# A four-stage graph and expert network on one core: the search for entries above one moves from the first stage to the last, and the general path moves behind it

## What is computed

```python
x = x + L0_gnn(layernorm(x), adj)   # e = leaky_relu(f1_i + f2_j); where(adj > 0, e, -9e15); softmax; @ h; elu
x = x + L0_ffn(layernorm(x))        # 8 experts, the best 2 for each row, gelu, hidden 256
x = x + L1_gnn(layernorm(x), adj)   # alpha = where(adj == k, leaky_relu((h * a_{k-1}) @ h.T), -9e15) for k = 1..4; softmax; @ h
x = x + L1_ffn(layernorm(x))        # 8 experts for every row, three products, weights from the mean over the batches
```

## Time and profile before

| what | us |
|---|---|
| three runs | 1109.86, 1111.55, 1112.64 (median 1111.55) |
| the profiled execution | 1111.38 |
| its span, first to last instruction | 1109.6 |
| stage A (0 to about 290), B (to 456.1), C (460.65 to 757.1), D (757.2 to the end) | 290, 166, 296, 352 |
| busy PE, PEld, DVE, ACT, POOL | 1028.1, 745.1, 685.0, 766.2, 383.6 |

### The profile page before, as it was taken

How to read it: one execution, slowest core, us unless ns; L and a number is a source line. 1 busy time by engine, 2 the same in 40 slices (tenths; PEclk the granted TensorE clock), 3 DMA queues, 4 the chain that set the end, 5 groups by cost and what they waited for, 6 DMA issues and landing times. The chain is left out here.

```text
span 1109.6 us, 20053 instructions
## 1 busy us (share of the span) xinstructions
PE 1028.1 (93%) x6445; PEld 745.1 (67%) x6445; DVE 685.0 (62%) x2172; ACT 766.2 (69%) x1176; POOL 383.6 (35%) x468
## 2 busy tenths in 40 slices
PE   4888889788899988699999999999999999999998
PEld 4556556555477777478888888886566666666667
DVE  5678898778564354388999899763533333333335
ACT  4998889776565545488888888885655656556551
POOL 4123788877572412556565653201000000000000
PEclk9899999999999999899999999999999999999999
DMA  8967997713246663323333322110000000000001
GB/s 302 347 270 277 389 335 272 282 47 126 79 144 228 203 182 116 111 68 86 87 92 93 89 85 74 58 30 1 1 11 10 10 20 10 10 20 10 10 19 30
DMA packets 70731, 128.53 MB, mean 116 GB/s; under 512 B 10095, under 2 KB 36317, under 8 KB 69597
## 3 DMA queue, kind: packets, MB, share of 16 engines
q1 hardware_dynamic: 61852, 109.34, 29.3%
q0 software_dynamic: 8192, 16.79, 5.0%
q10 hardware_dynamic: 576, 1.05, 0.2%
HBM read 76.69 MB, written 50.46 MB: 115 GB/s over the span
## 5 line engine op out<-in xcount | busy, mean ns | idle before, releaser
L2430 PEld LDWEIGHTS eY<-Vo,dGW 128*128 128x128 f32 x1024 | 132.3, 192 | 54.5 <-issue 52.8
L589 POOL DMA_INDIRECT sorted_x<-V,AT_I x128 | 125.6, 981 | 55.8 <-issue 36.7
L2430 PE MATMUL eY<-Vo,dGW 128*128 128x128 f32 x1024 | 134.3, 276 | 0.4 <-DVE dGW L2600 0.3
L2600 DVE TENSOR_TENSOR dGW<-H,WBC 128x512 f32<-128x512 f32 x80 | 55.3, 692 | 125.3 <-PE eY L2430 125.1
L2413 PE MATMUL eU<-XTN,V 128*128 128x512 f32 x256 | 130.9, 594 | 0.9 <-PEq L2348 0.9
L2421 PE MATMUL eU<-H,V 128*128 128x512 f32 x256 | 131.2, 594 | 0.0
L778 PE MATMUL O<-Y,HS 128*128 128x512 f32 x256 | 129.2, 625 | 0.0
L2031 POOL DMA_INDIRECT W<-sorted_y,ROW_I x96 | 96.8, 1009 | 70.5 <-PE f_T L2105 50.6
L2509 ACT ACTIVATE H<-eU,bn 128x512 f32<-128x512 f32 x128 | 99.5, 777 | 25.5 <-PE eU L2413 16.2
L2132 PEld LDWEIGHTS f_O<-f_XN,f_PT 128*128 128x128 f32 x896 | 106.8, 192 | 12.8 <-DVE X L2243 10.4
L2132 PE MATMUL f_O<-f_XN,f_PT 128*128 128x128 f32 x896 | 109.8, 276 | 2.6 <-DVE X L2243 2.0
(11 more groups left out here) (329 smaller groups left out, 2078.6 us busy)
## 6 DMA issues: line engine op xcount, KB each, us to landing
XTN<-in_adj SPq DMA_DIRECT2D x64, 512.0 KB, 5.5
masks<-NMW SPq DMA_DIRECT2D x8, 2048.0 KB
f_MK<-masks SPq DMA_DIRECT2D x60, 256.0 KB, 2.8
sorted_y<-zero SPq DMA_DIRECT2D x36, 256.0 KB
NMW<-sorted_x SPq DMA_DIRECT2D x25, 256.0 KB, 2.7
sorted_y<-NMW SPq DMA_DIRECT2D x25, 256.0 KB
X<-in_x SPq DMA_DIRECT2D x8, 512.0 KB, 7.1
out_x<-X SPq DMA_DIRECT2D x16, 256.0 KB, 2.3
```

What stands on the lines that cost most here:

```text
L589: g_.indirect_dma_start(sorted_x, bass.IndirectOffsetOnAxis(ap=AT_I[b % 2][:, kt:kt + 1], axis=0), XR[b % 2][:, t * P:(t + 1) * P], None). ...
L2430: i = pe.matmul(Y[q][:, t * P:(t + 1) * P], GW[:, j % 2, t * P:(t + 1) * P], Vo[:, e * P:(e + 1) * P], start=(e == 0 and t == 0), stop=(e ...
L2600: v.tensor_tensor(GW[:, j % 2, :], h2(j), WBC[:, e, q * HALF:(q + 1) * HALF], ALU.mult).then_inc(gw_ready, 1)
```

## The change

1. **Masks.** `look`, `seen` and `excess` go from stage A. Every `convert` on DVE reads the integers and writes 0 or +2^55, and PE takes them away with a negative identity (`minusb`) in place of adding them. The converts of the next batch, which stood in steps c = 2 (four tiles), 5 and 6 (two each), stand in c = 0 (two), 2 (three), 6 (one) and 7 (two); in batch 0 they stay in c = 3 to 6. `BY_VECTOR` is 8, so ACT's own `convert` loop is empty. SP's loads wait for the masks alone.
2. **Registers in stage B.** The experts for k >= 25 are read one at a time on DVE, between `finish(k - 1)` and `second_weights(k + 1)`.
3. **Kept rows.** SP stores every batch's x to memory (`keep_x`, 8 transfers of 512 KB): seven at k = 9 to 15 of stage B, that of batch 0 at its end, and there it waits until it has landed.
4. **No branch before C.** `one_kind` runs always.
5. **Search in stage D.** SP loads `adj` again (64 transfers of 512 KB, four buffers `entries`), DVE takes the maximum of each (`look(n)`, one 128x1024 `tensor_reduce`, from j = 10 on, in six of eight steps), the maximum of these at j = 108 and the flag at j = 124, with one transpose on PE.
6. **The branch at the end.** All engines load the flag behind stage D. If it is set, x is loaded back, and the general path and stage D run (again); if not, they only wait for the last stores. Semaphores that both paths share get other pairings, and C's `add` of the mask on DVE becomes a subtraction.

The diff, cut to these:

```diff
@@ stage A, SP and PE
                     for t in range(NT):
-                        if b == 1:
-                            sp.wait_ge(nm_ready, t + 1)
-                        sp.wait_ge(looked, (b - 1) * NT // 2 + t // 2 + 1)
+                        masks_due(sp, b - 1, t)
...
                             if c == 0:
-                                pe.wait_ge(nm_ready, b * NT + r + 1)
+                                masks_due(pe, b, r)
                             pe.matmul(t[:, r * P:(r + 1) * P], NM[:, b % 2, r, c * P:(c + 1) * P],
-                                      identb[:, :], start=(r % 4 == 0), stop=False)
+                                      minusb[:, :], start=(r % 4 == 0), stop=False)
@@ stage B, SP
+                def keep_x(b):
+                    for h in range(2):
+                        sp.wait_ge(x_added[h], b + 1)
+                    sp.dma_start(kept_x[b, :, :], X[:, b * N:(b + 1) * N]).then_inc(kept, 16)
...
+                    if RING < k < RING + B:
+                        keep_x(k - RING)
                 for k in range(NB - 6, NB):
                     store(k)
+                sp.wait_ge(x0_done, X0_MEANS)
+                keep_x(0)
+                sp.wait_ge(kept, 16 * 2 * B)
@@ stage A, ACT
-                    nc.scalar.activation(seen[:, n % 2, :, :], ADJ[:, 2 * k:2 * k + 2, :], ACT.Exp, bias=minus150[:, :], scale=100.0,
-                                         accum_out=excess[:, n:n + 1]).then_inc(looked, 1)
@@ stage A, DVE
                 def convert(b, t):
-                    n = (b * NT + t) // 2
-                    if b == 0:
-                        dve.wait_ge(adj_loaded[t], 16)
-                    else:
-                        dve.wait_ge(looked, n + 1)
+                    dve.wait_ge(adj_loaded[t], 16 * (b + 1))
...
-                    v.tensor_scalar(NM[:, b % 2, t, :], ADJ[:, t, :] if b == 0 else seen[:, n % 2, t % 2, :], 0.0, BLOCKED, ALU.is_le,
+                    v.tensor_scalar(NM[:, b % 2, t, :], ADJ[:, t, :], 0.0, -BLOCKED, ALU.is_le,
                                     ALU.mult).then_inc(nm_ready, 1)
...
-                        for t in (((), (), (), (0, 1), (2, 3), (4, 5), (6, 7), ()) if b == 0 else ((), (), (0, 1, 2, 3), (), (), (4, 5), (6, 7), ()))[c]:
+                        for t in (((), (), (), (0, 1), (2, 3), (4, 5), (6, 7), ()) if b == 0 else ((0, 1), (), (2, 3, 4), (), (), (), (5,), (6, 7)))[c]:
                             convert(b + 1, t)
@@ stage B, DVE
                 for k in range(NB):
-                    done, e = e, expert(k + 1) if k + 1 < NB else None
+                    if k < WHOLES - 1:
+                        done, e = e, expert(k + 1)
+                    else:
+                        done, e = e, coming
                     if OTHERS <= k + 1 < NB:
                         first_weights(k + 1, e)
                     if k >= 1:
                         finish(k - 1, last)
+                    if k >= WHOLES - 2:
+                        coming = expert(k + 2) if k + 2 < NB else None
@@ stage D
+            free = [j for j in range(10, G) if j % E not in (3, 5)]
+            searched_at = {n: free[n] for n in range(B * NT)} if search else {}
+            MOST, FLAG = G - 20, G - 4
...
+                for n in range(B * NT if search else 0):
+                    if n >= 4:
+                        sp.wait_ge(searched, n - 3)
+                    sp.dma_start(entries[:, n % 4, :], adj[n // NT, n % NT * P:(n % NT + 1) * P, :]).then_inc(entry_loaded[n % 4], 16)
...
+                def look(n):
+                    dve.wait_ge(entry_loaded[n % 4], 16 * (B // 4 + n // 4 + 1))
+                    v.tensor_reduce(most[:, n:n + 1], entries[:, n % 4, :], AX_X, ALU.max).then_inc(searched, 1)
...
+                    if search and j == FLAG:
+                        dve.wait_ge(m_ps, 7)
+                        op(v.tensor_reduce, lone[:, :], M[0][0:1, 0:P], AX_X, ALU.max)
+                        v.tensor_scalar(flag[:, :], lone[:, :], 1.0, None, ALU.is_gt)
@@ behind stage D (before: between stage B and stage C, around edge_attention and one_kind)
+        several = nc.values_load(flag[:, :], min_val=0, max_val=1)
+        with nc.If(several > 0):
...
+        with nc.Else():
...
+                @block.sync
+                def _(sp):
+                    for q in range(2):
+                        sp.wait_ge(last_sems[f"e_stored{q}"], 16 * B)
```

204 lines of the change are left out of this document (128 added, 76 removed).

## The result

The changed kernel takes 1118.99 us (median; 1117.42 to 1120.77 in four runs) beside 1111.93 us for the kernel before in the same comparison. The ratio is 1.0059, with a 95% interval of 1.0043 to 1.0074. It is slower by 0.4 to 0.7%, where 1099.8 us, 1.1% faster, was forecast. The profiled execution of after is the shortest of its four (1117.42 us) and has a span of 1115.6 us, 6.0 more than before's 1109.6, so the two traces can be laid side by side and the 6 us found piece by piece.

The account below looks back on a forecast made before the run. ACT was taken to bound batch 0, DVE batches 1 to 6, PE and SP stage B's last part, PE stage D. Terms -4.7 - 9.9 + 0 + 0.6 + 2.4 = -11.6 gave 1099.8 us, range 1091.5 to 1108.5.

Parts of the forecast that it names:

- Batch 0: Stage A, first batch: without look, DVE's waits for ACT go and dearer converts are added, -9.0 us.
- The transfers: Rival for stage A, batch 0: DMA transfers bound it, so -2 us in place of -9; chance 0.10.
- Batches 1 to 6: Stage A: dearer integer converts on DVE, less the waits that go or absorb them, +4.3 us.
- so I price it at nothing: Stage A boundaries: PE's wait for masks of c = 7 is covered by DVE's choice of experts; uncovered 2 x 0.64 us.
- The 2.0 us that batch 5 was to take in: Stage A: DVE's waits for POOL's sends, in batch 5 and another, absorb 2.0 us of the dearer converts.
- Contention, the rival on the other side: Rival, batches 1 to 6: integer converts beside POOL take 1101 ns each, +22 us, 1121.9 us in all; chance 0.05.
- The registers: Stage B, work(24) to work(38): single register reads remove the first two PE stalls, -6.6 us, entered as -6.0.
- The third stall: Stage B: 2.95 us of PE from 433 us on goes too, POOL's gathers starting earlier by as much.
- I give back 0.6: Stage B: the seven 512 KB stores of kept rows share SP's queue in the registers' stretch, costing 0.6 us.
- Batch 0's rows at the end of B: End of stage B: storing batch 0's x and waiting for it, unhidden, 3.5 us landing plus 0.4 to issue.
- The end: Behind stage D: flag load of 0.49 us and PE's jump of 3.85 us, partly beside the last store's landing, +2.4 us.
- The search: Stage D: 64 DVE reductions of 1.2 us each hide in DVE's waits for PE, 0 us.

Follow-up runs that it names:

- the two versions with all mends: Changed kernel with POOL's drain in stage D's block, kept rows on ACT's queue at k = 17 to 23, batch 0's earlier; two masks on ACT 1105.06 us, four 1090.72.

## Why the prediction was wrong, point by point

**What bounds the kernel** was read rightly for batch 0, batches 1 to 6 and stage D. It was read wrongly for stage B: SP was named as setting the pace only in the last part. In `work(11)` to `work(16)` PE was full in the trace of before and the issues of SP lay 4.3 to 4.8 us apart, so SP was already losing on PE. A busy engine hid that another had no slack.

**Batch 0**, -9.0: right, -9.3, with the mechanism named. The transfers did not bound it, though their share in 22 to 57 us rose from 0.94 to 1.02.

**Batches 1 to 6**, +4.3: the sign was right and the size was not (+8.2). Batch 2 shows the terms. Its converts cost 8 x 0.265 = 2.1 us more (a median of 685 ns for 420), where 1.85 had been taken. Of DVE's waits 0.8 us were to go; they grew by 0.5, because 1.30 came at the boundary. 2.1 + 0.5 is the 2.65 us by which the batch is longer. The step that failed is "so I price it at nothing", on PE's new wait for the masks made in c = 7. The cover that it named was there, and what it left out is PE's clock, which was on no line of the sum. The run with the kept rows at k = 17 to 23 settles this: its stage A has the same code, and at the boundary ahead of its batch 2 PE's clock did not fall. PE, then DVE's second `shift`, then the window:

```profile
78.12 0.23 PE L779 MATMUL T<-minusb,NMW 128*128 128x128 bf16 x1 [2.71 <-DVE NMW L1093]
...
78.84 1.94 PE L793 MATMUL O<-Y,HS 128*128 128x512 f32 x4
```

```profile
83.13 1.22 DVE L1149 CUSTOM_DVE_ANT_0 Y<-T,R 128x1024 f32<-128x1024 f32 x1
```

```profile
78.00:81.00 3.00, 2.57 (x15) 1.35 (x16) 2.79 (x11) 1.96 (x2) 0.00 (x0) 1.00 0.63 176
```

PE's gap is as long as in after, but the four products take 1.94 us, DVE has no wait at its second `shift`, and batch 2 takes 33.3 us, 1.3 more than before, where the prediction had 1.05. At the full clock it was nearly right. In that run's batches 3 and 4, where the clock is low for longer, the wait is 2.31 us. So the 1.28 us that the prediction gave for a wait without cover meets the 1.30 by chance. The trace of before had such a fall: the granted clock is 0.63 in 125 to 128 us, and PE had waited 2.07 us for ACT until 125.25. The 2.0 us that batch 5 was to take in were right: DVE's wait for POOL there is 0.83 us for 3.07. Contention, the rival on the other side, is refuted: of 64 converts the median is 685 ns and all but one take 814 or less. The one of 1099 is the third convert of the program, and it is as long in every trace, before's too. With that the lock on the shared ports, as the Trainium skill has it (page "SBUF — State Buffer", section on the two separate sides), is not seen to cost anything on these converts as a rule.

**The registers**, -6.0 for the first two stalls: the mechanism was right and the term too large, since 3.6 came. Blocks behind them run at 2.4 to 3.1 us for a while, not 2.15. The third stall gave its 2.9 us at the end of B, as forecast; with the registers alone the whole gain is 6.6 us.

**The kept rows** are the step that failed most. The prediction put the seven stores "on SP in that same stretch" as the registers, and "I give back 0.6". They stand at k = 9 to 15, where SP had no slack, and cost 8.3 us. What the stores cost was SP's time, for their issue and for the register loads beside it.

**Batch 0's rows at the end of B**: 3.5 us for the landing was somewhat large (2.8 from issue to landing), and most of it was needless: with the store three lines higher in the code, the stretch from `work(45)` to C is 7.0 us (kept rows on SP) or 5.3 (on ACT's queue) in place of 8.6. Why the two differ is not settled.

**The end**, +2.4: the flag load and PE's 3.85 us were right (3.57); with the drain hidden the end is 3.0 us longer than before. The term that is missing is POOL's drain, 4.5 us. The sum asked what each engine has to do behind stage D, and not what a block does at its end and where that had been hidden before.

**The search**, 0: right, 1.21 us a reduction as taken.

Put together: the sum was -11.6 and the span came out +6.0. Of the difference of 17.6 us, 8.3 are the kept rows, 5.1 the end, 3.9 batches 1 to 6 and 2.4 the first two stalls; the smaller terms together came out 2.1 better than forecast.

## What to carry to other kernels

Before a transfer is added to a queue, look at how far apart that queue's own issues lie against the step of the engine that it feeds: a queue that is slower than its consumer lives on a lead, and every issue that is added comes out at the other end in full. When a block becomes the last, or stops being the last, look up what it does when it closes, on every engine, and what covered that. And when work goes from a relieved engine to the one that bounds, count it there in full: with four masks on each engine `work(0)` came 15.8 us earlier than before the change, with all eight on DVE 2.4.

## What the runs showed of the hardware

- POOL's drain at the end of a block took 7.92 us (behind the branch) and 9.63 us (under stage D), with nothing else queued on POOL.
- A register load on SP mostly took 0.26 to 0.28 us, but single ones up to 1.01 in before already. Right behind a store of kept rows it took 0.54 (`FROM`) and 0.87 (`NEED`), and up to 1.24 us (`TO`) where the stores came from ACT's queue. Why it becomes longer is not settled. The busy share of the DMA engines alone does not tell it: in after they were 0.75 busy in 341 to 357 us, and the median read of `TO` took 0.27.
- Behind gaps of 2.65 and 2.72 us PE's granted clock fell to 0.68 to 0.75 over the next 3 to 6 us; behind one of 1.77 us in the same place two products took 1.02 us, as at the full clock, in place of 1.91. Behind one of 2.94 us in that place, and one of 2.71 us at a batch's boundary, it stayed at 1.00. So the length of a gap does not settle by itself whether the clock falls, and the same code had batches of 33.3, 34.7 and 37.6 us.
- A convert of 128x1024 integers took 0.685 us on DVE and 1.14 us on ACT. PE's jump took 3.34 to 3.87 us over all traces; it was not longer over the general path and a second stage D (after, 3.57) than over the general path alone (before, 3.85). ACT and DVE went on 3.7 and 3.6 us behind their own jumps in after, and POOL and SP 0.4 to 0.5.
- Not settled: why `work(0)` to `work(11)` took 52.2 and 50.4 us with two masks on ACT and 48.0 with four, why the stretch before `work(0)`, where PE waits for the first sorted rows, varied between 7.9 and 11.6 us, and why stage C took 295.0 us in place of 296.5 in the two versions with all mends.
